# Other counts of filling products at the waits of TensorE, 262 before and 254 after

## The reference

```python
x = _layernorm(x + _L0_attn_ref(x, ...))        # Nystrom attention, 16 heads, 64 landmarks,
                                                # pseudo-inverse in 6 iterations
x = _layernorm(x + _L0_xattn_ref(x, ctx, ctx))  # dilated attention in 3 branches
x = _layernorm(x + _L0_ffn_ref(x, ...))         # ternary weights, gelu
x = _layernorm(x + _L1_attn_ref(x, ...))        # memory with decay
x = _layernorm(x + _L1_xattn_ref(x, ctx, ctx))  # gated attention over two key sets, rope
x = _layernorm(x + _L1_ffn_ref(x, ...))         # top 2 of 8 experts
```

```python
out = attn1 @ (attn2_inv @ (attn3 @ v))         # of the first layer
```

## Time and profile before

| | before |
|---|---|
| median of three runs | 1688.19 us |
| range of the three | 1686.45 to 1689.84 us |
| profiled execution, its time | 1695.37 us |
| profiled execution, span | 1693.3 us |
| PE busy | 1430.2 us, 84% |
| DVE busy | 1095.3 us, 65% |
| ACT busy | 652.5 us, 39% |
| mean granted clock of PE | 0.934 |

### The profile page before, as it was taken

One profiled execution on the slowest core, in us unless ns is written; L12 is line 12 of the kernel. 1 busy time (PEld: TensorE's weight loads), 2 busy tenths in 40 slices (PEclk: granted clock), 3 DMA queues, 4 the chain that ended last, 5 costly groups with the idle time before them and its releaser, 6 DMA issues. The chain is left out here.

```text
span 1693.3 us, 45878 instructions
## 1 busy us (share of the span) xinstructions
PE 1430.2 (84%) x19556; PEld 1162.7 (69%) x19588; DVE 1095.3 (65%) x2483; ACT 652.5 (39%) x1349; POOL 296.7 (18%) x335
## 2 busy tenths in 40 slices
PE   5997996779898777898996879988773899999993
PEld 4995773559776555796774549767542799999882
DVE  5776676556856846576677556756845565655874
ACT  3313444332144343213443323144341564555771
POOL 0002130120202202002130020202202012122232
PEclk8799998989999898899998989999996899999997
DMA  7331120010000001000000010000001878788844
GB/s 274 125 134 81 39 81 13 15 38 4 3 3 1 26 2 40 14 4 2 3 13 13 14 40 4 2 3 1 1 2 55 300 244 291 242 276 269 268 126 112
DMA packets 50385, 134.51 MB, mean 79 GB/s; under 512 B 5121, under 2 KB 28929, under 8 KB 49153
## 3 DMA queue, kind: packets, MB, share of 16 engines
q1 hardware_dynamic: 39993, 116.75, 19.4%
q0 software_dynamic: 7152, 9.57, 2.8%
q10 hardware_dynamic: 3040, 5.26, 0.8%
HBM read 117.80 MB, written 32.13 MB: 89 GB/s over the span
## 5 line engine op out<-in xcount | busy, mean ns | idle before, releaser
L739 PE MATMUL bank<-arena 64*64 64x80 f32 (+2 forms) x6400 | 222.7, 229 | 3.9 <-DVE arena L878 2.4
L739 PEld LDWEIGHTS bank<-arena 64*64 64x64 f32 x6400 | 216.5, 140 | 13.1 <-issue 7.2
L1058 POOL TENSOR_TENSOR rstd<-ve,neghalf 128x2 f32<-128x2 f32 x48 | 37.4, 779 | 717.5 <-DVE ve L1036 716.7
L2218 PE MATMUL m_bank<-e_xT,e_w 128*128 128x256 bf16 x1440 | 161.2, 274 | 2.1 <-DVE e_xT L2319 2.1
L2218 PEld LDWEIGHTS m_bank<-e_xT,e_w 128*128 128x128 bf16 x1440 | 141.5, 98 | 19.8 <-DVE e_xT L2319 2.9
L2314 DVE TENSOR_TENSOR e_w<-e_raw,e_w 128x1024 bf16<-128x1024 f32 x90 | 108.8, 1223 | 39.7 <-ACT e_w L2258 39.5
L2334 DVE TENSOR_TENSOR e_h<-m_bank,e_silu 128x256 f32<-128x256 f32 x120 | 50.7, 422 | 89.8 <-ACT e_silu L2279 89.8
L599 PE MATMUL bank<-c_bf 128*128 128x512 bf16 x230 | 72.8, 466 | 32.3 <-ACT arena L982 10.0
L2279 ACT ACTIVATE e_silu<-m_bank 128x256 f32<-128x256 f32 (+1 forms) x192 | 65.7, 344 | 86.8 <-PE m_bank L2218 79.6
L2258 ACT CAST e_w<-e_raw 128x1024 bf16<-128x1024 f32 x90 | 92.3, 1042 | 17.9 <-DMA e_raw<-E 17.9
L1002 ACT COPY arena<-bank 128x320 f32<-128x320 f32 (+1 forms) x96 | 37.5, 391 | 159.6 <-PE bank L739 159.3
(11 more groups left out here) (317 smaller groups left out, 2972.1 us busy)
## 6 DMA issues: line engine op xcount, KB each, us to landing
e_raw<-E SPq DMA_DIRECT2D x144, 512.0 KB, 8.8
slots<-C_empty SPq DMA_DIRECT2D x13, 1360.0 KB
e_x<-slots SPq DMA_DIRECT2D x15, 272.0 KB, 8.0
w_rest<-W_rest SPq DMA_DIRECT2D x1, 3592.0 KB, 16.7
xz<-xT SPq DMA_DIRECT2D x8, 256.0 KB, 2.7
x<-x SPq DMA_DIRECT2D x8, 256.0 KB, 2.9
ctx<-ctxT SPq DMA_DIRECT2D x8, 256.0 KB, 2.7
tokens<-y SPq DMA_DIRECT2D x8, 256.0 KB, 2.1
```

What stands on the lines that cost most here:

```text
L739: last = pe.matmul(b[r, p * width:(p + 1) * width], lhs[r, 4 * g + p, :], rhs[r, 4 * g + p, :], start=True, stop=True)
L2218: last = pe.matmul(bank[b][:, col:col + wide], w, x, start=j == 0, stop=j == len(terms) - 1)
```

## The change

Only the table changes. Every other line is the same, so no engine but PE has another instruction, and PE has the same ones in the same order but for the counts of fills. The core of the diff:

```diff
-    "n_max1_0": "00909090",
-    "n_aT_0": "00909090",
-    "n_xT": "09090909",
+    "n_max1_0": "00929292",
+    "n_aT_0": "02300030",
+    "n_xT": "010011010011",
+    "r_xT": "00000004",
     "g_m00_0": "09090909",
-    "g_negT": "90909090",
-    "n_negT": "90000000",
+    "g_negT": "90907080",
+    "n_negT": "90000001",
+    "d_total": "00000002",
...
-    "d_s0_0": "01010101",
-    "g_s01_0": "10101010",
-    "g_o0": "30202020",
-    "g_o1": "03030303",
-    "m_xT": "06050509",
+    "d_s0_0": "01010100",
+    "d_s2_0": "00000200",
+    "g_s00_0": "20000000",
+    "g_s01_0": "10303035",
+    "g_s10_0": "00002010",
+    "g_s11_0": "01101010",
+    "g_o0": "30505050",
+    "g_o1": "01030303",
+    "m_xT": "06050559",
```

## The result

Time after: **1699.1 us**, median of 5 runs (1695.52 to 1702.88), against 1689.84 (1686.45 to 1691.73, 5 runs) for the kernel before beside it. The ratio is 1.0055 with an interval of 1.0037 to 1.0073, so +9.3 us (+6 to +12). Forecast were 1692.3 and a range of 1683.5 to 1697.5. The direction was right, but the sum had +4.1 us where +9.3 came, and the time lies outside the range. Of the 6.8 us between 1692.3 and 1699.1, 1.65 are in the kernel before, whose median was 1688.19 when the forecast was made and 1689.84 beside the change.

What follows compares the result with a forecast made beforehand. The layers were taken as bound by a chain passing between PE, DVE and ACT. Terms of +1.2, -1.0, +3.9, -1.3, +1.8 and -0.5 sum to +4.1 us, for a median of 1692.3 us, range 1683.5 to 1697.5.

Steps and rivals of the forecast that it cites:

- n_xT, +3.9: Fewer fills at n_xT: 3.1 us idle, clock falls behind it, +1.3 us each in b1, b3, b5; b7 paid already.
- The prediction's end of 9.1: Upper end at n_xT: two low stretches of 1.3 us at each of four places, less the one there now.
- n_aT_0, +1.2: Nine fills become 3, 0, 3 in b2, b4, b6: +0.4 us each, ends -5.6 and +4.0.
- the row of b0: At n_aT_0 of b4 without fills: the two products take b0's 8.75 us in place of 8.36, +0.4.
- the low end: At n_aT_0 of b2 and b6 with three fills, clock low throughout: 10.0 us, +1.8.
- n_max1_0, -1.0: Two fills more in b3, b5, b7 may keep the clock from falling: -1.0 us, between -3.9 and +0.5.
- g_negT -1.3: Nine fills become 7 and 8 in b4 and b6: three fills of 0.42 us less on the path.
- m_xT -0.5: Five fills at m_xT of b6 may keep the clock up: -0.5 us, ends -1.5 and +0.4.
- small additions +1.8: Added fills where PE does not idle or overrun short idle time: half of 3.6 us, ends 0 and +3.6.
- Fills were plain delay: Rival: L729 at n_aT_0 runs at the high level's pace with three or no fills; -6.6 us, 1681.6, chance 0.19.
- The low stretches only move: Rival: low clock stretches come elsewhere, where PE waits anyway; 0 to +2.5 us, say 1689.5, chance 0.31.
- All low: Rival: L729 low behind three fills, two low stretches at the n_xT places; +9 us, about 1698, chance 0.12.

Runs made afterwards that it cites:

- e5_after: The changed kernel as it is, timed again beside the kernel before on chip Q: ratio 1.0037, +6.3 us.
- h4_both: Kernel before with only the changed entries of n_xT, n_aT_0 and n_max1_0, on chip R: ratio 0.9983, -2.8 us.
- i1_after_again: The changed kernel once more, beside the kernel before on chip S: ratio 0.9991, -1.5 us.
- g4_best: Changed kernel with n_xT's nine fills back and 6 fills at g_negT of b2, b4, b6, against before on chip Q: ratio 1.0034, +5.7 us.
- i2_mx9_at0: Before with 6 fills at g_negT of b2, b4, b6, 9 at m_xT of b0, b2, b4, b6, none at n_aT_0, chip S: -10.7 us.
- e2_at: Kernel before with only the changed entries of n_aT_0 and n_max1_0, on chip P: ratio 0.9964, -6.0 us.
- e7_at0: Kernel before with no fills at n_aT_0 of b2, b4 and b6, on chip Q: ratio 1.0007, +1.2 us.

## Why the prediction was wrong in size, step by step

- **n_xT, +3.9: the step that failed.** The mechanism was right in each of its signs: 3 us idle, the level down, the product at 3.7 us, the chain longer to its end. Its price was too low. It was that of one low stretch of 3.4 us, 1.3 us in b7, taken in three rounds; but after, b1, b3 and b7 have 6.8 us at 0.50 in this stretch. The row that the prediction itself called the nearest for an idle time of that length, m_xT, has 6.7 us, so the row of the price was the wrong one. With the stall, which is the case forecast, the four profiles with 0, 1 or 5 fills have 220.1 us behind n_xT in the mean and the four with nine 213.9: +6.2. The times of the entry alone agree, +6.9 (+3.7 to +10.1) with one or no fill and +5.7 with five. Without the stall it is 219.6 against 215.4, +4.3, and +3.5 in time. The prediction's end of 9.1 covered all of these. As a sentence apart: the Trainium skill, page "TensorE: Matmul & The Clock Gate", section "Terms", puts the penalty at half the throttled time; the four stretches have 23.8 us at 0.50 after and 3.4 before, which by it is an estimate of 10.2 us more, and the trace has 7.2, so this rule of thumb lies above the measurement, as the prediction's term lay below it.
- **n_aT_0, +1.2.** The size was about right, the places were not. From the first fill (L722 in b4; the first fill, which isn't recorded, set one fill of 0.42 us ahead of the row) to the end of L735 the three places took 7.32, 8.95 and 10.35 us, where before had 8.33, 8.42 and 8.27: +1.6. b4 went by the row of b0, as forecast, b6 by the low end, b2 gained.
- **n_max1_0, -1.0.** Nothing was bought: the level was low in all three rounds. L663 starts 0.8 us behind L735's end, where L657 followed at once, and L745, which waits for DVE too, 1.33 us behind it in place of 1.14. Over several profiles the two terms together come to nothing with the stall (354.5 against 354.7), where the sum had +0.2; the +4.7 of the first pair of profiles is that of two single executions.
- **g_negT -1.3, m_xT -0.5, small additions +1.8.** The first two came out at -1.6 and -0.4 in the trace. The third was not measured by itself; all three together took +0.2 and +2.8 without the stall, neither apart from 0, where the sum had 0.0.
- **The sum.** With 6.2 in place of 3.9 it is +6.4, beside +6.3 in e5_after (+3 to +9.5). The +4.1 as forecast lies inside that interval and outside the first one, +6 to +12. So part of the miss of the first measurement may be chance, and n_xT is the one term that several runs show to be too small.
- **Adding up.** The sum took the terms as independent, and did not say so. Without the stall they add within the error (h4_both -2.8 against -3.2; i1_after_again -1.5 against -2.3). With it g4_best, at +5.7 where -1 to -3 was expected, shows that they need not.
- **The rivals.** "Fills were plain delay" was called against by the trace, and for that chip rightly. Its deciding point, whether the clock is up when L729 starts, is the one on which the chips differ. Its gain did come without the stall with three, no and three fills (-6.0, -7.4), but not with none at all (i2_mx9_at0). "The low stretches only move" has a part: executions of one kernel differ by 8 to 17 us on Q, and the two profiles of the changed kernel with the stall differ by 6.0 us behind n_aT_0. "All low" described b4 and b6 and three of the four places n_xT, and its 1698 was nearest.
- **The range and the chances.** 1697.5 cut the outer half of "All low". What was known of the level when it was set (low throughout in b0, up behind the fills in b2, low for 6.7 us behind the idle time at m_xT) gave no ground for halving that case. And by its own parts the prediction's chance of slower is 0.12 and three quarters of 0.38, about 0.40, and that of the same 0.41, not the 0.47 and 0.34 that it states.

What stays open: what lets the four indirect DMAs hold up the updates on one chip and not on others, and how the low levels hand on from one place to the next, which must be known to say why g4_best lost 5.7 us; and which of the entries at n_aT_0 and n_max1_0 gains without the stall.

## What to carry to other kernels

Products that only fill a wait are worth their time by what stands ahead of them: read the idle time that the engine has just had, and the length of the same products with and without them, at each place. Nine fills inside 3.1 us of idle time that no one can use were worth 0.9 to 1.7 us a round at n_xT (3.5 to 6.9 over four), and 1.8 us at m_xT of b0; of five no worth was seen. Follow the time to the end of the round: what is saved at a place can be lost again in the stretch behind it, as in i2_mx9_at0. A table of such counts should not be tuned on one chip alone, nor by single profiles: the same kernel took 6.3 us more than before on one chip, and no more than before on another (-1.5). When a row is picked for a price, take it for its cause (how long PE idled) and not for its place in the program.

## What the runs showed of the hardware that was not expected

- Beside four indirect DMAs of POOL the semaphore updates of the other engines stayed out for 3.6 to 4.9 us (ACT's L982 idle 4.69 us, "remote"), three times in a run, in the first profiles and in all six on chip Q that have the DMAs; without the DMAs and their waits it was gone. On three other chips no profile has it, and the kernel before took 1673 to 1675 us in place of 1688 to 1690. A releaser named "remote" beside work that was long done was the mark of it in these profiles.
- With these DMAs left out Q came to 1673.8 us, the level of the other chips.
- L729 without fills took 3.76 us behind 0.79 us of idling in e2_at's b4 and 7.04 behind 3.00 us in e7_at0's b2. The idle time alone does not decide it: in b0 of before it took 7.04 behind 0.57 us, at a level that was low already, and in i2_mx9_at0's b2 5.44 behind 0.79.
